# A second layer norm's statistics on ACT, and the softmax denominator's sum and reciprocal on POOL

## The chip, the cores and the metric

The kernel runs on one core of a Trainium2 chip. Its engines are named as the profile names them: PE (TensorE, matmuls and transposes), DVE (VectorE), ACT (ScalarE), POOL (GpSimd) and SP (SyncE, which issues the DMAs). Each works through its own queue in the order written, and waits on semaphores for the others. The metric is the device time of one execution in microseconds (us), the median of three timed runs.

## What is computed

The input is x of 8 x 1024 x 128. Each of the two halves of the block normalises, works, and adds a gated result to x. In the reference, cut to what matters here:

```python
h = _layernorm(x, axis=-1) * (1 + ca) + sa
# for each of 8 heads of 16 columns, over a causal window of 64 positions:
dist = sqrt((diff * diff * m_h).sum(-1) + 1e-08); dist = where(mask, dist, inf)
neg_d, loc = top_k(-dist, 32)
infl = exp(-topd)
infl = infl / (infl.sum(axis=-1, keepdims=True) + 1e-08)        # the softmax denominator
context = einsum('btk,btkd->btd', infl, neighbor_v)
context = context + gate * 0.1 * heb_ctx
out = q_h * context
x = x + ga * (out_sparse @ decoder)
h = _layernorm(x, axis=-1) * (1 + cb) + sb                      # the second layer norm
x = x + gb * _L0_ffn_ref(h, ...)
```

with `_layernorm(x) = (x - mean) / sqrt(var + 1e-5)` over the 128 columns.

## The kernel before, in words

A first part (to about 100 us) normalises x, makes the transposed projections of all 8192 rows and keeps them in SBUF. The main part goes over 64 chunks (`NCH`) of 128 rows each. Each engine has its own `step(i)`, called for i from -3 to 66, in which `k = i + off` names the chunk that an operation works on: several chunks are under way at once. `there(i, off)` says whether that chunk exists, and `s`, `s4` are its buffer of two or of four. The order of the work on each engine is written out by hand by the order of these blocks; nothing reorders it.

One chunk goes this way. SP copies rows into `hst`, `tst`, `sst`. PE multiplies `sqs` and `selm` into norms (L1239, L1241, group `pn`), which ACT copies to `nst` (L752) and `n2` (L758). PE's `distances` (L1149, L1152) fill PSUM; ACT takes two relus of them (L666, L667), DVE joins the third piece into `key` (L998), ACT raises `key` by Ln and Exp (L701, L719). DVE then picks the 32 nearest of each 64 by four rounds of MAX8 (`maxes`, L965) and MATCH_REPLACE8 (`replaces`, L976) for eight heads, into `work`. ACT squares and exponentiates `work` by halves (L628, L635), POOL unfolds it (`big`, L452), PE transposes it (L1168), ACT copies it (L642), PE multiplies it with the values into the contexts (L1182). ACT copies these by two halves of the partitions to `cst` (L713, L714).

In `cst` the last column of each head, `cst[:, s, :, HD]`, is the softmax's sum of weights. DVE adds 1e-8 to it (`den`, L1013) and takes the reciprocal (`rden`, L1026). POOL makes `t1` = context times q (L481), `t2` = the Hebbian part (L483, L485), later `t1` times `rden` (L461) and `osp` = their sum (L465). PE transposes it (L1199) and multiplies with the decoder onto x (L1209, L1210), and ACT copies that sum to `x2` (L706). Then comes the second layer norm: DVE takes BN_STATS (`st_c`, L1007) and BN_AGGR (`mv_c`, L1019), which gives mean and variance of each row; ACT makes `lv_c` = Ln(var + eps), `nm_c` = -mean, `rs_c` = Exp(-lv/2), `nb_c` = nm times rs and `n_c`, the normalised rows (L724, L725, L727, L740, L746). PE transposes them (L1251), ACT scales them to `h2T` (L658), PE multiplies with the chunk's expert matrix (L1190, L1191), ACT copies the result to `yo` (L673) and SP stores it.

On POOL, behind `t1` and `t2`, stand `selm` (L491, an operand of the norms of chunk i + 3), `hsc` (L497), `sst` (L502) and two operations on `n2` (L509, L510).

Of the kernel before, what the change touches and what calls it, by code (L numbers as in the profile page):

```python
# [7 lines left out]
ALU = mybir.AluOpType  # L8
ACT = mybir.ActivationFunctionType
# [4 lines left out]
P = 128  # L14
NB, T, D = 8, 1024, 128
NH, HD = 8, 16
# [13 lines left out]
EPS_LN = 1e-5  # L30
# [47 lines left out]
def adaln_block(nc, x, encq, encv, w1, b1, w2, b2, base, hebu, hebv, dec, wr, amat, bmat, cin, wmod, consts, out):  # L78
    ctx = ExitStack()

    def sb(name, shape, dt=F32):
        return ctx.enter_context(nc.sbuf_tensor(name, shape, dt))

    def sem(name):
        return ctx.enter_context(nc.semaphore(name))

    with ctx:
# [20 lines left out]
        unf = con[:, C_UNF:C_UNF + 2 * WIN].rearrange("p (v j) -> p v j", v=2)  # L108
        ident_bf = sb("ident_bf", [P, P], BF16)
        mask_bf = sb("mask_bf", [P, SW], BF16)  # L110
        bias = sb("bias", [P, 4])

        hT_all = sb("hT_all", [P, NB * TP])
        qT_all = sb("qT_all", [P, NG, NB * TP])
# [48 lines left out]
        den = sb("den", [P, 2, NH])  # L163
# [11 lines left out]
        oT = sb("oT", [P, 2, CH])  # L175
        xs = sb("xs", [P, 4, D])
        x2 = sb("x2", [P, 2, D])
        st_c = sb("st_c", [P, 6])
        mv_c = sb("mv_c", [P, 2, 2])
        lv_c = sb("lv_c", [P, 1])  # L180
        nm_c = sb("nm_c", [P, 1])
        nb_c = sb("nb_c", [P, 1])
# [115 lines left out]
        att_ready = sem("att_ready")  # L298
        xs_in = [sem(f"xs_in{i}") for i in range(4)]
        x2_ready = sem("x2_ready")  # L300
        stc_ready = sem("stc_ready")
        mvc_ready = sem("mvc_ready")
        lnc_done = sem("lnc_done")
        nc_ready = sem("nc_ready")
        pn2_ready = sem("pn2_ready")
# [5 lines left out]
        def need(eng, s, value):  # L311

            if value > 0:
                eng.wait_ge(s, value)
# [12 lines left out]
        def there(i, off):  # L327

            return 0 <= i + off < NCH
# [70 lines left out]
        def _(pool):  # L400
# [5 lines left out]
                ins.then_inc(pool_chain, 1)  # L406
                pool.wait_ge(pool_chain, links[0])

            for col, value in enumerate((EPS_LN, 1e-8, 1.0, 0.0)):
                nc.gpsimd.memset(bias[:, col:col + 1], value).then_inc(bias_set, 1)  # L410
            nc.gpsimd.memset(udiag[:], 0.0).then_inc(ones_set, 1)
            for s in range(4):
# [31 lines left out]
            def step(i):  # L444
                def unfold(w):

                    k, s = i - 1, (i - 1) % 2
                    if there(i, -1):
                        need(pool, wt_ready, 8 * (k - 2) + 4 * w + 4)
                        pool.wait_ge(wsel_ready, 2 * k + 1 + w)  # L450
                        heads = slice(4 * w, 4 * w + 4)
                        nc.gpsimd.tensor_tensor(  # L452
                            wun[:, s, heads].rearrange("p h (v j) -> p h v j", v=2),
                            work[:, s].rearrange("p (h j) -> p h j", h=NH)[:, heads].unsqueeze(2).broadcast_to([P, 4, 2, WIN]),
                            unf.unsqueeze(1).broadcast_to([P, 4, 2, WIN]), ALU.mult).then_inc(w_ready, 1)

                k, s = i - 2, (i - 2) % 2
                if there(i, -2):
                    pool.wait_ge(rden_ready, k + 1)
                    pool.wait_ge(t1_done, k + 1)  # L460
                    nc.gpsimd.tensor_tensor(t1[:].rearrange(h3, h=NH), t1[:].rearrange(h3, h=NH), rden[:, s].unsqueeze(2).broadcast_to([P, NH, HD]), ALU.mult).then_inc(ctx_done, 1)  # L461
                    need(pool, po_ready, k - 1)
                    pool.wait_ge(t2_done, 2 * (k + 1))
                    pool.wait_ge(ctx_done, k + 1)
                    nc.gpsimd.tensor_tensor(osp[:, s], t1[:], t2[:], ALU.add).then_inc(osp_ready, 1)  # L465

                unfold(0)

                unfold(1)

                k, s = i + 3, (i + 3) % 2
                if there(i, 3):
                    win = qT_all[:, :, bass.ds(column(k), 3 * WIN)]
                    need(pool, pn_ready, k - 1)
                    nc.gpsimd.tensor_tensor(sqs[:, s], win, win, ALU.mult).then_inc(opnd_ready, 1)

                k, s, s4 = i - 1, (i - 1) % 2, (i - 1) % 4
                if there(i, -1):
                    q, hb = qh[:, s4, :, 0:HD], qh[:, s4, :, HD:2 * HD]
                    pool.wait_ge(cst_ready, 2 * (k + 1))  # L480
                    nc.gpsimd.tensor_tensor(t1[:].rearrange(h3, h=NH), cst[:, s, :, 0:HD], q, ALU.mult).then_inc(t1_done, 1)  # L481
                    pool.wait_ge(hsc_done, k + 1)
                    nc.gpsimd.tensor_tensor(t2[:].rearrange(h3, h=NH), hb, hsc[:, s].unsqueeze(2).broadcast_to([P, NH, HD]), ALU.mult).then_inc(t2_done, 1)  # L483
                    pool.wait_ge(t2_done, 2 * k + 1)
                    nc.gpsimd.tensor_tensor(t2[:].rearrange(h3, h=NH), t2[:].rearrange(h3, h=NH), q, ALU.mult).then_inc(t2_done, 1)  # L485

                k, s = i + 3, (i + 3) % 2
                if there(i, 3):
                    if i == FIRST:
                        pool.wait_ge(aS_ready, 1)  # L490
                    nc.gpsimd.tensor_tensor(selm[:, s], seln, aS[:, :, bass.ds(k // CPB, 1)].broadcast_to([P, NG, NH]),  # L491
                                            ALU.mult).then_inc(opnd_ready, 1)

                k, s, s4 = i, i % 2, i % 4
                if there(i, 0):
                    pool.wait_ge(rnn_ready, k + 1)
                    nc.gpsimd.tensor_tensor(hsc[:, s], gat[:, s4], rnn[:, s], ALU.mult).then_inc(hsc_done, 1)  # L497

                k, s = i + 3, (i + 3) % 2
                if there(i, 3):  # L500
                    need(pool, dist_ready, k - 1)
                    nc.gpsimd.tensor_tensor(sst[:, s, :, 0:3 * WIN], qT_all[:, :, bass.ds(column(k), 3 * WIN)],  # L502
                                            aS[:, :, bass.ds(k // CPB, 1)].broadcast_to([P, NG, 3 * WIN]), ALU.mult).then_inc(s_ready, 1)

                k, s4 = i + 2, (i + 2) % 4
                if there(i, 2):
                    need(pool, n2_ready, k + 1)
                    need(pool, rnn_ready, k - 3)
                    nc.gpsimd.tensor_scalar(gat[:, s4], n2[:, s4], GATE2, 0.1, ALU.is_gt, ALU.mult).then_inc(n2g_ready, 1)  # L509
                    nc.gpsimd.tensor_scalar(n2g[:, s4], n2[:, s4], 1e-18, None, ALU.max).then_inc(n2g_ready, 1)  # L510
# [15 lines left out]
        def _(act):  # L526
# [1 line left out]
            act.wait_ge(c_in, 32)  # L528

            nc.scalar.activation(ec[:], c_sb[:], ACT.Exp, scale=-1.0).then_inc(ec_ready, 1)  # L530
            act.wait_ge(bias_set, 4)

            def logvar(n, u):
                act.wait_ge(mv_ready, 4 * n + 4)
# [87 lines left out]
            def step(i):  # L622
# [80 lines left out]
                k, s = i - 2, (i - 2) % 2  # L703
                if there(i, -2):
                    act.wait_ge(att_ready, k + 1)
                    nc.scalar.activation(x2[:, s], pAtt, ACT.Copy).then_inc(x2_ready, 1)  # L706

                k, s = i - 1, (i - 1) % 2
                if there(i, -1):
# [3 lines left out]
                    nc.scalar.activation(cst[0:WIN, s], pc[0:WIN, :, 0], ACT.Copy).then_inc(cst_ready, 1)  # L713
                    nc.scalar.activation(cst[WIN:P, s], pc[WIN:P, :, 1], ACT.Copy).then_inc(cst_ready, 1)  # L714

                k, s = i + 1, (i + 1) % 2
                if there(i, 1):
                    act.wait_ge(ln_done, k + 1)
# [1 line left out]

                k, s = i - 2, (i - 2) % 2
                if there(i, -2):
                    act.wait_ge(mvc_ready, k + 1)
                    nc.scalar.activation(lv_c[:], mv_c[:, s, 1:2], ACT.Ln, bias=bias[:, 0:1]).then_inc(lnc_done, 1)  # L724
                    nc.scalar.activation(nm_c[:], mv_c[:, s, 0:1], ACT.Copy, scale=-1.0).then_inc(nm_done, 1)  # L725
                    act.wait_ge(lnc_done, k + 1)
                    nc.scalar.activation(rs_c[:, s:s + 1], lv_c[:], ACT.Exp, scale=-0.5).then_inc(rs_done, 1)  # L727

                k, s4 = i + 2, (i + 2) % 4
                if there(i, 2):  # L730
# [4 lines left out]

                k, s = i - 2, (i - 2) % 2
                if there(i, -2):
                    act.wait_ge(nm_done, k + 1)
                    act.wait_ge(rs_done, k + 1)
                    nc.scalar.activation(nb_c[:], nm_c[:], ACT.Identity, bias=bias[:, 3:4], scale=rs_c[:, s:s + 1]).then_inc(nb_done, 1)  # L740

# [22 lines left out]
        def _(dve):  # L764
# [214 lines left out]
            def step(i):  # L979
# [21 lines left out]
                replaces(i, 2, 0)  # L1001
                replaces(i, 2, 1)

                k, s = i - 2, (i - 2) % 2
                if there(i, -2):
                    dve.wait_ge(x2_ready, k + 1)
                    v.bn_stats(st_c[:], x2[:, s]).then_inc(stc_ready, 1)  # L1007

                k, s = i - 1, (i - 1) % 2
                if there(i, -1):  # L1010
                    dve.wait_ge(cst_ready, 2 * (k + 1))
                    need(dve, rden_ready, k - 1)
                    v.tensor_scalar(den[:, s], cst[:, s, :, HD], 1e-8, None, ALU.add).then_inc(den_done, 1)  # L1013

                k, s = i - 2, (i - 2) % 2
                if there(i, -2):
                    need(dve, stc_ready, k + 1)
                    need(dve, nc_ready, k - 1)
                    v.bn_aggr(mv_c[:, s], st_c[:]).then_inc(mvc_ready, 1)  # L1019

                maxes(i, 3)
                replaces(i, 3, 0)
                k, s = i - 1, (i - 1) % 2
                if there(i, -1):
                    dve.wait_ge(den_done, k + 1)
                    v.reciprocal(rden[:, s], den[:, s]).then_inc(rden_ready, 1)  # L1026

                replaces(i, 3, 1)

            steps(step, routing)  # L1030
# [269 lines left out]
```

## Time and profile before

| | |
|---|---|
| median of 3 timed runs | 841.48 us (840.1 to 842.94) |
| the profiled execution | 845.14 us, of which the span of instructions is 843.4 |
| busy, share of the span | DVE 94%, PE 85%, ACT 73%, PEld 70%, POOL 55% |
| granted TensorE clock, mean | 0.958 |
| main part, from the first `st_c` to the slow tail | 126.0 to about 805 us |
| one repetition (one chunk) there | 11.32 us |

Busy time is the time in which an engine has an instruction of its own under way; PEld is PE's loading of weights, beside its matmuls. A row of a timeline gives the start in us from the start of the span, the time it took, engine, line, operation and operands, and in brackets how long the engine was idle before it and which engine's instruction released it. Instructions on DVE, ACT and POOL overlap a little at their ends, so that two starts can be closer than the first instruction is long. In the last 38 us the granted clock of PE is half, which the page's line on the clock shows.

### The profile page before, as it was taken

What the parts mean: (1) busy time and instruction counts of PE and PEld (TensorE: products, weight loads), DVE (VectorE), ACT (ScalarE), POOL (GpSimd) and SP (SyncE); (2) the same over time, 40 slices, a digit from 0 to 9 for tenths busy, and PEclk for the clock granted to TensorE, in tenths of its full rate; (3) what the DMA queues carried; (4) which work ended last, traced back from release to release, by engine and by line L of the source; (5) the groups of instructions that cost most, each with busy time, mean ns of one, the idle gap of its engine ahead of it and who ended that gap; (6) DMA issues with size and microseconds to landing.
All of it is one profiled execution on the core that took longest, in us unless ns stands there. A gap on an engine that the chain in (4) does not pass through costs nothing.

```text
span 843.4 us, 21229 instructions
## 1 busy us (share of the span) xinstructions
PE 718.6 (85%) x4437; PEld 586.2 (70%) x4437; DVE 788.9 (94%) x6746; ACT 619.5 (73%) x1862; POOL 463.0 (55%) x871
## 2 busy tenths in 40 slices
PE   5997989888888888888888888888888888888845
PEld 3445677777777777777777777777777777777744
DVE  5855999999999999999999999999999999999980
ACT  3981368787777878777777877777878777787853
POOL 2112456666556566655656665565566655656541
PEclk9996989999999999999999999999999999999955
DMA  5310001101111110011110001111100111111000
GB/s 165 102 32 10 24 24 30 30 20 32 31 31 31 29 30 24 27 31 30 32 30 29 26 24 32 31 31 30 30 29 21 31 31 31 31 30 30 18 4 9
DMA packets 49232, 27.24 MB, mean 32 GB/s; under 512 B 5512, under 2 KB 48592, under 8 KB 49104
## 3 DMA queue, kind: packets, MB, share of 16 engines
q1 hardware_dynamic: 49104, 25.90, 10.4%
q8 instruction: 36, 0.59, 0.3%
q14 instruction: 92, 0.75, 0.3%
HBM read 10.28 MB, written 4.19 MB: 17 GB/s over the span
## 4 chain that ended last, share of the span: by engine, by line
DVE 83%; PE 10%; DMA 2%; ACT 2%; issue 2%; POOL 1%; SPq 1%; ACTq 0%; POOLq 0%
DVE work L976 44%; DVE m L965 29%; DVE key L998 4%; DMA big<-in_x 2%; DVE st_c L1007 1%; PE psD L1152 1%; DVE mv_c L1019 1%; PE psC L1182 1%; DVE key L787 1%; PE psD L1057 1%; DVE st_p L778 1%; PE psC L1085 1%; PE psW L1239 1%; DMA wmod_sb<-in_wmod 1%; PE psW L1168 1%
## 5 line engine op out<-in xcount | busy, mean ns | idle before, releaser
L976 DVE MATCH_REPLACE8 work<-m,work 128x64 f32<-128x64 f32 x1536 | 301.8, 208 | 0.0
L1152 PE MATMUL psD<-sst,tst 128*128 128x224 f32 x1024 | 238.9, 356 | 0.0
L965 DVE MAX8 m<-work 128x8 f32<-128x64 f32 x1536 | 209.9, 209 | 0.0
L1152 PEld LDWEIGHTS psD<-sst,tst 128*128 128x128 f32 x1024 | 196.3, 192 | 3.2 <-issue 0.3
L452 POOL TENSOR_TENSOR big<-work,con 128x512 f32<-128x512 f32 x128 | 162.2, 1291 | 13.0 <-ACT work L635 12.9
L481 POOL TENSOR_TENSOR t<-cst,qh 128x128 f32<-128x128 f32 x64 | 27.8, 434 | 232.3 <-ACT cst L714 232.3
L1182 PE MATMUL psC<-vst,big 128*128 128x34 f32 x1024 | 129.0, 272 | 0.0
L1182 PEld LDWEIGHTS psC<-vst,big 128*128 128x128 f32 x1024 | 128.4, 197 | 0.2
L976 DVE MATCH_VALUE_LOAD work<-m,work 128x8 f32 x1536 | 120.0, 78 | 0.0
L976 DVE MATCH_REPLACE8 work<-m,key 128x64 f32<-128x64 f32 x512 | 100.2, 208 | 0.0
L1149 PE MATMUL psD<-mask_bf,ident_bf 128*128 128x448 bf16 x256 | 91.1, 356 | 9.3 <-DMA tst<-nst 1.8
L701 ACT ACTIVATE key<-key,bias 128x512 f32<-128x512 f32 x64 | 46.2, 721 | 69.5 <-DVE key L998 69.5
L1168 PE MATMUL psW<-con,big 128*128 128x128 f32 x512 | 80.0, 280 | 2.9 <-POOL big L452 2.9
L642 ACT ACTIVATE big<-psW 128x512 f32<-128x512 f32 x128 | 76.1, 595 | 3.1 <-PE psW L1168 3.0
L1239 PE MATMUL psW<-sqs,selm 128*8 128x192 f32 x256 | 53.4, 332 | 22.6 <-POOL selm L491 22.6
L965 DVE MAX8 m<-key 128x8 f32<-128x64 f32 x512 | 70.4, 208 | 0.0
L1190 PE MATMUL psX<-x,con 128*128 128x128 f32 x128 | 32.5, 337 | 37.1 <-ACT h2T L658 37.1
L724 ACT ACTIVATE lv_c<-mv_c,bias 128x1 f32<-128x1 f32 x64 | 18.8, 294 | 59.9 <-DVE mv_c L1019 59.9
L1168 PEld LDWEIGHTS psW<-con,big 128*128 128x128 f32 x512 | 58.5, 144 | 4.4 <-POOL big L452 4.1
L1190 PEld LDWEIGHTS psX<-x,con 128*128 128x128 f32 x128 | 19.9, 195 | 59.2 <-ACT h2T L658 59.2
L502 POOL TENSOR_TENSOR sst<-qT_all,aS 128x384 f32<-128x384 f32 x64 | 53.1, 829 | 12.7 <-PE psD L1152 12.7
L635 ACT ACTIVATE work<-work 128x256 f32<-128x256 f32 x128 | 53.3, 417 | 4.1
(199 smaller groups left out, 1474.7 us busy)
## 6 DMA issues: line engine op xcount, KB each, us to landing
hst<-hT_all SPq DMA_DIRECT2D x64, 96.0 KB
tst<-qT_all SPq DMA_DIRECT2D x256, 17.0 KB
big<-in_x SPq DMA_DIRECT2D x16, 256.0 KB, 2.8
tst<-nst SPq DMA_DIRECT2D x256, 1.0 KB
xs<-in_x SPq DMA_DIRECT2D x64, 64.0 KB, 1.9
out<-yo SPq DMA_DIRECT2D x64, 64.0 KB, 1.7
sst<-nst SPq DMA_DIRECT2D x128, 3.0 KB
con<-in_consts SPq DMA_DIRECT2D x1, 549.5 KB, 5.8
```

The source lines that it names most:

```text
L452: nc.gpsimd.tensor_tensor(wun[:, s, heads].rearrange("p h (v j) -> p h v j", v=2), work[:, s].rearrange("p (h j) -> p h j", h=NH)[:, heads ...
L502: nc.gpsimd.tensor_tensor(sst[:, s, :, 0:3 * WIN], qT_all[:, :, bass.ds(column(k), 3 * WIN)], aS[:, :, bass.ds(k // CPB, 1)].broadcast_to( ...
L635: nc.scalar.activation(wk, wk, ACT.Exp, scale=-1.0).then_inc(wsel_ready, 1)
L642: nc.scalar.activation(wts[:, (i - 1) % 2, 4 * w:4 * w + 4].rearrange("p h t -> p (h t)"), psW[:, w], ACT.Copy).then_inc(wts_ready, 1)
L965: last = v.max(m8[:, h], src[:, h * WIN:(h + 1) * WIN])
L976: last = v.match_replace(work[:, s, cols], m8[:, h], src[:, cols], GONE)
L1149: mm(bank_of(r)[:, :, 0:SW], ident_bf[:], mask_bf[:].unsqueeze(1).broadcast_to([P, NG, SW]), start=True, stop=False, skip_group_check=True)
L1152: last = mm(bank_of(r)[:, g, 0:SW], tst[:, s, r, g], sst[:, s, g], start=False, stop=(g == NG - 1), skip_group_check=True)
L1168: nc.tensor.transpose(psW[:, w, (h % 4) * P:(h % 4 + 1) * P], wun[:, s, h], ident).then_inc(wt_ready, 1)
L1182: last = mm(pC[:, h * 2 * VD:(h + 1) * 2 * VD], wts[:, s, h], vst[:, s4, h].rearrange("p v e -> p (v e)"), start=True, stop=True)
L1190: mm(pY, ident, x2[:, s], start=True, stop=False)
L1239: mm(pN, selm[:, s, g], sqs[:, s, g], start=(g == 0), stop=(g == NG - 1))
```

## The change

The second layer norm's statistics are no longer taken on DVE. ACT's copy to `x2` becomes an Identity with `accum_out`, which gives the sum of the row; `nm_c` = -sum/128; a new ACTIVATE `Square` of `x2` with bias `nm_c` and `accum_out` gives the sum of squares about the mean, `ssq_c`, and `lv_c` = Ln(ssq/128 + eps). The pieces `nm_c`, `Square`, `lv_c`, `rs_c` are spread over three places between the copies of `cst` and `n_c`. An ACTIVATE with `accum_out` is followed by a second instruction that reads the accumulator, as the two at L565 in the first part are. The softmax's `den` goes to POOL, ahead of `t1`; its reciprocal becomes a TENSOR_TENSOR with the operation `pow` against a column of -1, on POOL behind `t1`. One more memset makes that column. PE's and SP's code is unchanged.

```diff
@@ pool, step
                     pool.wait_ge(cst_ready, 2 * (k + 1))
+                    need(pool, ctx_done, k - 1)
+                    nc.gpsimd.tensor_scalar(den[:, s], cst[:, s, :, HD], 1e-8, None, ALU.add).then_inc(den_done, 1)
                     nc.gpsimd.tensor_tensor(t1[:].rearrange(h3, h=NH), cst[:, s, :, 0:HD], q, ALU.mult).then_inc(t1_done, 1)
+                    pool.wait_ge(den_done, k + 1)
+                    nc.gpsimd.tensor_tensor(rden[:, s], den[:, s], bias[:, 4:5].broadcast_to([P, NH]), ALU.pow).then_inc(rden_ready, 1)
                     pool.wait_ge(hsc_done, k + 1)
@@ act, step
                     act.wait_ge(att_ready, k + 1)
-                    nc.scalar.activation(x2[:, s], pAtt, ACT.Copy).then_inc(x2_ready, 1)
+                    nc.scalar.activation(x2[:, s], pAtt, ACT.Identity, bias=bias[:, 3:4],
+                                         accum_out=sum_c[:, s:s + 1]).then_inc(x2_ready, 1)
...
+                    act.wait_ge(x2_ready, k + 1)
+                    nc.scalar.activation(nm_c[:], sum_c[:, s:s + 1], ACT.Copy, scale=-1.0 / D).then_inc(nm_done, 1)
...
-                    act.wait_ge(mvc_ready, k + 1)
-                    nc.scalar.activation(lv_c[:], mv_c[:, s, 1:2], ACT.Ln, bias=bias[:, 0:1]).then_inc(lnc_done, 1)
-                    nc.scalar.activation(nm_c[:], mv_c[:, s, 0:1], ACT.Copy, scale=-1.0).then_inc(nm_done, 1)
-                    act.wait_ge(lnc_done, k + 1)
-                    nc.scalar.activation(rs_c[:, s:s + 1], lv_c[:], ACT.Exp, scale=-0.5).then_inc(rs_done, 1)
+                    act.wait_ge(nm_done, k + 1)
+                    nc.scalar.activation(sq_c[:], x2[:, s], ACT.Square, bias=nm_c[:], accum_out=ssq_c[:]).then_inc(ssq_done, 1)
...
-                    act.wait_ge(nm_done, k + 1)
+                    act.wait_ge(ssq_done, k + 1)
+                    nc.scalar.activation(lv_c[:], ssq_c[:], ACT.Ln, bias=bias[:, 0:1], scale=1.0 / D).then_inc(lnc_done, 1)
+                    act.wait_ge(lnc_done, k + 1)
+                    nc.scalar.activation(rs_c[:, s:s + 1], lv_c[:], ACT.Exp, scale=-0.5).then_inc(rs_done, 1)
@@ dve, step
-                    dve.wait_ge(x2_ready, k + 1)
-                    v.bn_stats(st_c[:], x2[:, s]).then_inc(stc_ready, 1)
...
-                    dve.wait_ge(cst_ready, 2 * (k + 1))
-                    need(dve, rden_ready, k - 1)
-                    v.tensor_scalar(den[:, s], cst[:, s, :, HD], 1e-8, None, ALU.add).then_inc(den_done, 1)
...
-                    need(dve, stc_ready, k + 1)
-                    need(dve, nc_ready, k - 1)
-                    v.bn_aggr(mv_c[:, s], st_c[:]).then_inc(mvc_ready, 1)
...
-                    dve.wait_ge(den_done, k + 1)
-                    v.reciprocal(rden[:, s], den[:, s]).then_inc(rden_ready, 1)
```

What stands in a row on POOL in a chunk of the main part, before, from `sqs` to `hsc`:

```order
L475 TENSOR_TENSOR sqs<-qT_all 128x384 [waits pn_ready]
L481 TENSOR_TENSOR t<-cst,qh 128x128 [waits cst_ready]
L483 TENSOR_TENSOR t<-qh,hsc 128x128 [waits hsc_done]
L485 TENSOR_TENSOR t<-t,qh 128x128 [waits t2_done]
L491 TENSOR_TENSOR selm<-con,aS 128x16
L497 TENSOR_TENSOR hsc<-gat,rnn 128x8 [waits rnn_ready]
```

and the same place on POOL now:

```order
L475 TENSOR_TENSOR sqs<-qT_all 128x384 [waits pn_ready]
L482 TENSOR_SCALAR den<-cst 128x8 [waits ctx_done,cst_ready]
L483 TENSOR_TENSOR t<-cst,qh 128x128
L485 TENSOR_TENSOR rden<-den,bias 128x8 [waits den_done]
L487 TENSOR_TENSOR t<-qh,hsc 128x128 [waits hsc_done]
L489 TENSOR_TENSOR t<-t,qh 128x128 [waits t2_done]
L495 TENSOR_TENSOR selm<-con,aS 128x16
L501 TENSOR_TENSOR hsc<-gat,rnn 128x8 [waits rnn_ready]
```

`selm` now has two more instructions between itself and `cst`.

On ACT, before, from the copy to `x2` to the first `Square` of the next chunk's `work`:

```order
L706 ACTIVATE x<-psX 128x128 [waits att_ready]
L713 ACTIVATE cst<-psC 64x136 [waits osp_ready,c_ready]
L714 ACTIVATE cst<-psC 64x136
L719 ACTIVATE key<-key 128x512 [waits ln_done]
L724 ACTIVATE lv_c<-mv_c,bias 128x1 [waits mvc_ready]
L725 ACTIVATE nm_c<-mv_c 128x1
L727 ACTIVATE rs_c<-lv_c 128x1 [waits lnc_done]
L733 ACTIVATE vst<-psW 128x16x16 [waits c_ready,v_ready]
L740 ACTIVATE nb_c<-nm_c,bias,rs_c 128x1 [waits rs_done,nm_done]
L746 ACTIVATE n_c<-x,nb_c,rs_c 128x128 [waits pn2_ready,nb_done]
L752 ACTIVATE nst<-psW 8x192 [waits rows_in1,pn_ready]
```

and the same place on ACT now:

```order
L710 ACTIVATE x,sum_c<-psX,bias 128x128 [waits att_ready]
L718 ACTIVATE cst<-psC 64x136 [waits osp_ready,c_ready]
L719 ACTIVATE cst<-psC 64x136
L724 ACTIVATE nm_c<-sum_c 128x1 [waits x2_ready]
L729 ACTIVATE key<-key 128x512 [waits ln_done]
L734 ACTIVATE sq_c,ssq_c<-x,nm_c 128x128 [waits nm_done]
L740 ACTIVATE vst<-psW 128x16x16 [waits c_ready,v_ready]
L746 ACTIVATE lv_c<-ssq_c,bias 128x1 [waits ssq_done]
L748 ACTIVATE rs_c<-lv_c 128x1 [waits lnc_done]
L750 ACTIVATE nb_c<-nm_c,bias,rs_c 128x1 [waits rs_done]
L756 ACTIVATE n_c<-x,nb_c,rs_c 128x128 [waits pn2_ready,nb_done]
L762 ACTIVATE nst<-psW 8x192 [waits rows_in0,pn_ready]
```

`Square` has come in, `lv_c` and `rs_c` stand behind `vst`, and the wait for `mvc_ready` is gone.

## Rows read from the trace of the kernel before

**Rows 1.** Windows: one repetition; PE, PEld, DVE, ACT, POOL busy; clock; DMA share; GB/s.

```profile
408.91:420.23 11.32, 9.94 (x67) 8.41 (x66) 11.32 (x103) 8.90 (x27) 7.00 (x14) 1.00 0.10 30
```

**Rows 2.** The page's chain that ended last, by engine.

```profile
DVE 83%; PE 10%; DMA 2%; ACT 2%; issue 2%; POOL 1%; SPq 1%; ACTq 0%; POOLq 0%
```

**Rows 3.** That chain in order of time: start, time in the chain, engine, line.

```profile
408.91 0.20 DVE st_c L1007
409.11 0.07 DVE den L1013
409.18 0.15 DVE mv_c L1019
...
411.10 0.06 DVE rden L1026
...
420.23 0.20 DVE st_c L1007
```

**Rows 4.** Timeline of ACT over one repetition.

```profile
399.95 0.40 ACT L628 ACTIVATE work<-work 128x256 f32<-128x256 f32 x1
...
405.17 0.21 ACT L696 ACTIVATE rnn<-lnn 128x8 f32<-128x8 f32 x1
406.38 0.72 ACT L701 ACTIVATE key<-key,bias 128x512 f32<-128x512 f32 x1 [1.00 <-DVE key L998]
407.01 0.26 ACT L706 ACTIVATE x<-psX 128x128 f32<-128x128 f32 x1
407.17 0.26 ACT L713 ACTIVATE cst<-psC 64x136 f32<-64x136 f32 x1
407.46 0.28 ACT L714 ACTIVATE cst<-psC 64x136 f32<-64x136 f32 x1
...
409.36 0.29 ACT L724 ACTIVATE lv_c<-mv_c,bias 128x1 f32<-128x1 f32 x1 [0.98 <-DVE mv_c L1019]
...
411.01 0.30 ACT L752 ACTIVATE nst<-psW 8x192 f32<-8x192 f32 x1
...
411.27 0.40 ACT L628 ACTIVATE work<-work 128x256 f32<-128x256 f32 x1
```

**Rows 5.** Timeline of POOL and PE in the same repetition.

```profile
405.53 0.98 PE L1182 MATMUL psC<-vst,big 128*128 128x34 f32 x8
...
407.81 0.44 POOL L481 TENSOR_TENSOR t<-cst,qh 128x128 f32<-128x128 f32 x1 [3.55 <-ACT cst L714]
...
409.10 0.21 POOL L491 TENSOR_TENSOR selm<-con,aS 128x16 f32<-128x16 f32 x1
...
409.37 0.82 PE L1239 MATMUL psW<-sqs,selm 128*8 128x192 f32 x4 [0.37 <-POOL selm L491]
...
410.11 0.61 PE L1241 MATMUL psW<-con,sqs 128*128 128x8 f32 x4
```

**Rows 6.** All `st_c` (first and last start), and one `den` in the slow tail.

```profile
L1007 DVE BATCH_NORM_STATS2 st_c<-x x64: 273/284/298, 126.0 to 836.6; 128x6 f32<-128x128 f32 x64
...
817.33 0.17 DVE L1013 TENSOR_SCALAR den<-cst 128x8 f32<-128x8 f32 x1 [1.50 <-ACT cst L714]
```

**Rows 7.** Groups of instructions: count | busy us, mean ns of one | idle before.

```profile
L658 ACT ACTIVATE h2T<-psX,modT 128x128 f32<-128x128 f32 x64 | 28.2, 441 | 1.2 <-PE psX L1251 1.1
L565 ACT ACTIVATION_READ_ACCUMULATOR qT_all<-psD,con 128x1 f32 x32 | 7.0, 220 | 0.0
L497 POOL TENSOR_TENSOR hsc<-gat,rnn 128x8 f32<-128x8 f32 x64 | 13.0, 204 | 0.0
L509 POOL TENSOR_SCALAR gat<-n 128x8 f32<-128x8 f32 x64 | 16.2, 253 | 5.7 <-ACT n L758 0.4
L452 POOL TENSOR_TENSOR big<-work,con 128x512 f32<-128x512 f32 x128 | 162.2, 1291 | 13.0 <-ACT work L635 12.9
L965 DVE MAX8 m<-work 128x8 f32<-128x64 f32 x1536 | 209.9, 209 | 0.0
L965 DVE MAX8 m<-key 128x8 f32<-128x64 f32 x512 | 70.4, 208 | 0.0
```

More of the change, by code:

```diff
@@ L110, in adaln_block @@
         mask_bf = sb("mask_bf", [P, SW], BF16)
-        bias = sb("bias", [P, 4])
+        bias = sb("bias", [P, 5])
         hT_all = sb("hT_all", [P, NB * TP])
@@ L177, in adaln_block @@
         x2 = sb("x2", [P, 2, D])
-        st_c = sb("st_c", [P, 6])
-        mv_c = sb("mv_c", [P, 2, 2])
+        sum_c = sb("sum_c", [P, 2])
+        ssq_c = sb("ssq_c", [P, 1])
+        sq_c = sb("sq_c", [P, D])
         lv_c = sb("lv_c", [P, 1])
@@ L300, in adaln_block @@
         x2_ready = sem("x2_ready")
-        stc_ready = sem("stc_ready")
-        mvc_ready = sem("mvc_ready")
+        ssq_done = sem("ssq_done")
         lnc_done = sem("lnc_done")
@@ L407, in link @@
                 pool.wait_ge(pool_chain, links[0])
-            for col, value in enumerate((EPS_LN, 1e-8, 1.0, 0.0)):
+            for col, value in enumerate((EPS_LN, 1e-8, 1.0, 0.0, -1.0)):
                 nc.gpsimd.memset(bias[:, col:col + 1], value).then_inc(bias_set, 1)
@@ L530, in _ @@
             nc.scalar.activation(ec[:], c_sb[:], ACT.Exp, scale=-1.0).then_inc(ec_ready, 1)
-            act.wait_ge(bias_set, 4)
+            act.wait_ge(bias_set, 5)
             def logvar(n, u):
@@ L714, in step @@
                     nc.scalar.activation(cst[WIN:P, s], pc[WIN:P, :, 1], ACT.Copy).then_inc(cst_ready, 1)
+                k, s = i - 2, (i - 2) % 2
+                if there(i, -2):
+                    act.wait_ge(x2_ready, k + 1)
+                    nc.scalar.activation(nm_c[:], sum_c[:, s:s + 1], ACT.Copy, scale=-1.0 / D).then_inc(nm_done, 1)
                 k, s = i + 1, (i + 1) % 2
@@ L1002, in step @@
                 replaces(i, 2, 1)
-                k, s = i - 2, (i - 2) % 2
-                if there(i, -2):
-                    dve.wait_ge(x2_ready, k + 1)
-                    v.bn_stats(st_c[:], x2[:, s]).then_inc(stc_ready, 1)
-                k, s = i - 1, (i - 1) % 2
-                if there(i, -1):
-                    dve.wait_ge(cst_ready, 2 * (k + 1))
-                    need(dve, rden_ready, k - 1)
-                    v.tensor_scalar(den[:, s], cst[:, s, :, HD], 1e-8, None, ALU.add).then_inc(den_done, 1)
-                k, s = i - 2, (i - 2) % 2
-                if there(i, -2):
-                    need(dve, stc_ready, k + 1)
-                    need(dve, nc_ready, k - 1)
-                    v.bn_aggr(mv_c[:, s], st_c[:]).then_inc(mvc_ready, 1)
                 maxes(i, 3)
                 replaces(i, 3, 0)
-                k, s = i - 1, (i - 1) % 2
-                if there(i, -1):
-                    dve.wait_ge(den_done, k + 1)
-                    v.reciprocal(rden[:, s], den[:, s]).then_inc(rden_ready, 1)
                 replaces(i, 3, 1)
```

## Prediction

> **What bounds the kernel now.** I read four views, in this order. First the busy time of the engines over one repetition in the middle of the run. DVE is busy 11.32 of 11.32 us there, PE 9.94, ACT 8.90, POOL 7.00 [rows 1]. One repetition is the distance from one `st_c` to the next, 420.23 - 408.91 = 11.32 us [rows 3]. Second the chain that ended last by engine: 83% DVE [rows 2]. Third that chain in order of time: through the repetition it never leaves DVE, and the four instructions that the change takes away stand in it with 0.20 (`st_c`), 0.07 (`den`), 0.15 (`mv_c`) and 0.06 us (`rden`) [rows 3]. These are shares by which they hold up the next one, smaller than the instructions' own times because DVE starts the next before the last has ended. Fourth the timelines of ACT, POOL and PE, for how near the other engines are to a bound of their own [rows 4, 5]. So anything that shortens DVE pays at once, until the next loop through the other engines is as long.
>
> **What DVE gives up.** 0.20 + 0.07 + 0.15 + 0.06 = 0.48 us in each repetition. Nothing waits in their place: MAX and MATCH_REPLACE follow each other as they do in the other rounds. DVE alone could run at 11.32 - 0.48 = 10.84 us. The first `st_c` is at 126.0 [rows 6]; from there to 805, where the slow tail begins, are 60 repetitions of 11.32. The bound of the gain is 60 x 0.48 = 28.8 us.
>
> **What ACT takes.** ACT sits idle 1.00 us for `key` from DVE and 0.98 us for `mv_c` from DVE in each repetition [rows 4]. The second wait goes, for `nm_c` now comes from ACT's own sum. Added: the `x2` copy becomes an Identity with a bias column and a sum. An ACTIVATE with two columns is 0.44 long (`h2T`), the copy of the same size 0.26; with one column I take the middle, +0.1, and the read of the accumulator is 0.22 [rows 4, 7]. `Square` is a new 128x128 ACTIVATE of at most 0.44 with another 0.22. Together 0.1 + 0.22 + 0.44 + 0.22 = 1.0 us, and 8.90 + 1.0 = 9.9 is under 10.84. The four small ones (`nm_c`, `lv_c`, `rs_c`, `nb_c`) stay, and only move. What hides this work is the idle time that ACT has; were that gone, the 1.0 us would all show. On the order within ACT: `x2` stands ahead of the two `cst` copies and now delays them by about 0.3 - 0.1 = 0.2 us. In the repetition shown, the first `cst` starts at 407.17, while the products that it reads end at 405.53 + 0.98 = 406.51 [rows 4, 5], so it is ACT, not PE, that sets `cst` now.
>
> **What POOL takes, and the loop on which it lies.** POOL waits for the second `cst` until 407.81, and has its own idle time ahead of that (3.55 us) [rows 5]; by its busy share two small instructions are free. By its place they are not. Behind the new `den` and power stand `t1`, `t2` and `selm`; PE waits for `selm` (0.37 idle) before the norms' matmuls, ACT's `nst` copy waits for those, and on ACT the whole next repetition, `Square` of `work` first, queues behind `nst`. That closes a loop: work (ACT) - yo (ACT) - transposes and contexts (PE) - cst (ACT) - POOL - pn (PE) - nst - work. Its length with no wait for DVE in it, from the rows:
> from `work` at 399.95 to the end of the second half of the contexts at 406.51, 6.56 [rows 4, 5] (this stretch is dense: from ACT's `yo` on PE has no pause, and ACT's own way, 5.43 to the end of `rnn`, then 0.63 for `key`, 0.16 + 0.23 for `x2`, is 6.45 and hidden behind it); 0.05 to `cst`, 0.29 + 0.28 for the two copies: 7.18; 0.07 to POOL, then 409.10 + 0.21 - 407.81 = 1.50 to the end of `selm`: 8.75; 0.06 to PE, 410.11 + 0.61 - 409.37 = 1.35 for the norms: 10.16; 0.03 to `nst` and 411.27 - 411.01 = 0.26 to `work`: 10.45 us [rows 4, 5]. Before, this is 0.87 us under DVE's 11.32 and costs nothing. Now `den` adds the 0.25 of a TENSOR_SCALAR 128x8, less the 0.04 by which POOL's instructions overlap, 0.21; and the power adds p - 0.04, where p is its duration [rows 5, 7]. The loop becomes **10.62 + p**, against 10.84 for DVE.
>
> **The price of the power.** No power on any engine is in the trace. From below: the same shape with a multiply takes 0.20 us (`hsc`), p = 0.20 [rows 7]. From above, 16 times as many multiplies take 0.44 us (`t1`), 64 times as many 1.29 us (`unfold`) [rows 5, 7]. Less than 0.20 I exclude, since that is what POOL takes for the lightest operation of this shape. A power is many operations on each element; I take the row of 16 multiplies as nearest, p = 0.43, and keep 0.20 and 1.29 as ends. Then the loop is 11.05 us, longer than DVE's 10.84, and it sets the pace: 60 x (11.32 - 11.05) = 16.2 us gained.
>
> **The tail.** Behind 805 us the statistics chain of the last chunks lies bare, as DVE's wait of 1.50 us for `cst` shows [rows 6]. There about 0.35 us on DVE per chunk give way to the sum's read, `Square` and its read, 0.22 + 0.44 + 0.22, so some 0.5 us more, three times: +1.5 us. In the head nothing is removed from the chain that I can see. The sum for the profiled execution: span 843.4 - 16.2 + 1.5 = 828.7. It took 845.1 us, and the median of the three timed runs is 841.5; on that I put the difference of -14.7: **826.8 us**.
>
> **A rule that speaks against it.** MAX8 takes 209 ns when it reads `work` and 208 when it reads `key`, in rounds beside which POOL works and in rounds beside which it idles [rows 7], so POOL and DVE do not slow each other in the rows that count. The Trainium skill, page "Perfetto Trace Analysis", section "Optimizing Scalar/DVE Operations", warns that GpSimd and DVE share an SBUF read port, so that moving work between these two might not help. If it acted here the two tiny operations would lose part of DVE's gain; that is the contention rival below.
>
> **Rivals.** (1) DVE stays the bound. The power costs no more than 0.22 us: 10.84 us, 28.8 - 1.5 = 27.3 gained, 814.2 us. For it: 8 elements a partition, and the row of the multiply. Against: only if a power is as cheap as a multiply. Chance 0.22. (2) The power is dear, on the other side: one mechanism, POOL's `den` and power ahead of `selm`, from p = 0.68 on no gain is left (10.62 + 0.68 = 11.30, and the tail). At p = 1.29 the repetition is 11.91: 60 x 0.59 + 1.5 = +36.9, 878 us; at p = 1.0 it is 11.62, +19.5, 861 us. For it: POOL's order, and the 0.37 that PE already waits for `selm`. Against: POOL's fixed share dominates at 8 elements. Chance 0.27. (3) Between them, p from 0.63 to 0.72: within 2.5 us of 841.5; chance 0.08. (4) ACT or a port in the way: ACT's reads of the accumulator cost double, or DVE loses 0.1 to 0.2 us beside POOL. ACT has 10.84 - 9.9 = 0.9 us to spare, so it would have to be 1.9 us and not 1.0; for contention nothing in the rows speaks. It would come out at about 845; chance 0.05. My forecast, p from 0.22 to 0.63, has 0.38.
>
> **How the numbers follow.** A measurement of this kernel tells 0.3%, 2.5 us, from no change. Faster: 0.38 + 0.22 = 0.60. Same: 0.08. Slower: 0.27 + 0.05 = 0.32. The range goes from the DVE bound with 2 us to spare, 812, up to the power at 1.0 us, 860; beyond that I leave about 0.15.
>
> **What would show it.** Right: the repetition is 11.05 us, the distance between two `key` of DVE; DVE has a new wait of some 0.2 us a repetition, on ACT's `qh` or on `key`; ACT's wait for `mv_c` is gone, its wait for `key` nearly so, and there is a new one for `nst` from PE's norms; PE's wait for `selm` grows; the power's row reads about 0.43. Wrong in the first step: DVE is still without a pause, at 10.84. Wrong in the price: the power's row reads other than 0.43, and the repetition is off 10.62 + p. Wrong in the loop: the power's row is near 0.43 and the repetition is not near 11.05; then some stretch that I took as dense had slack in it, or ACT's added work is not hidden.

## The result and the profile after

The changed kernel takes 957.4 us, the median of four runs (955.4 to 959.0), against 842.2 us of the kernel before in runs beside it. The ratio is 1.137, 95% interval 1.133 to 1.141. It is 115.2 us slower; the forecast was 14.7 us faster, with 860 us as the upper end. Both the sign and the range were wrong.

The page of the kernel after: the span, the busy time, two of the lines in 40 slices, and the chain that ended last by engine ("issue" is time in which the engine waited for nothing that the profile shows).

```profile
span 957.0 us, 21168 instructions
...
PE 765.3 (80%) x4437; PEld 634.6 (66%) x4437; DVE 765.0 (80%) x6490; ACT 674.7 (71%) x2054; POOL 583.9 (61%) x1000
...
DVE  5957988888788888788888788787788888878880
...
PEclk9977899988899988899988899889888999988955
...
PE 47%; POOL 23%; ACT 15%; issue 9%; DVE 3%; DMA 2%; SPq 0%; POOLq 0%; ACTq 0%
```

DVE did become lighter, 765.0 us busy instead of 788.9, but it now idles and has 3% of the chain where it had 83% [rows 2]. Two things stand out. POOL is in the chain with 23%. And the granted clock of PE, which before stayed at full from 126 us to the tail, now reads 8 or 9 in the tenths of the page through the main part, 0.92 in the mean from 126 to 900 us.

The costliest groups and the waits of the kernel after (busy us, mean ns of one | idle before, releaser):

```profile
L485 POOL TENSOR_TENSOR rden<-den,bias 128x8 f32<-128x8 f32 x64 | 106.7, 1667 | 0.0
L1228 PE MATMUL psW<-sqs,selm 128*8 128x192 f32 x256 | 53.1, 330 | 105.9 <-POOL selm L495 105.9
L762 ACT ACTIVATE nst<-psW 8x192 f32<-8x192 f32 x64 | 20.5, 320 | 133.3 <-PE psW L1230 133.3
L1008 DVE SCALAR_TENSOR_TENSOR key<-psD,key 128x512 f32<-128x512 f32 x64 | 44.2, 691 | 133.7 <-ACT qh L690 133.6
```

The power takes 1667 ns. The three waits are the loop of the prediction, link by link: PE waits for `selm` from POOL, ACT waits with `nst` for PE, DVE waits with `key` for ACT's `qh`. Here is an undisturbed repetition, one in which PE's granted clock stays at full, on the timelines of POOL, PE, ACT and DVE:

```profile
404.06 0.25 POOL L482 TENSOR_SCALAR den<-cst 128x8 f32<-128x8 f32 x1 [4.10 <-ACT cst L719]
404.27 0.43 POOL L483 TENSOR_TENSOR t<-cst,qh 128x128 f32<-128x128 f32 x1
404.67 1.66 POOL L485 TENSOR_TENSOR rden<-den,bias 128x8 f32<-128x8 f32 x1
406.30 0.40 POOL L487 TENSOR_TENSOR t<-qh,hsc 128x128 f32<-128x128 f32 x1
...
407.19 0.22 POOL L495 TENSOR_TENSOR selm<-con,aS 128x16 f32<-128x16 f32 x1
...
407.46 0.82 PE L1228 MATMUL psW<-sqs,selm 128*8 128x192 f32 x4 [1.77 <-POOL selm L495]
...
408.86 0.32 ACT L762 ACTIVATE nst<-psW 8x192 f32<-8x192 f32 x1 [1.98 <-PE psW L1230]
...
413.56 0.69 DVE L1008 SCALAR_TENSOR_TENSOR key<-psD,key 128x512 f32<-128x512 f32 x1 [1.25 <-ACT qh L690]
...
425.75 0.69 DVE L1008 SCALAR_TENSOR_TENSOR key<-psD,key 128x512 f32<-128x512 f32 x1 [1.25 <-ACT qh L690]
```

From one `key` to the next are 12.19 us where a repetition took 11.32 [rows 3]. Sixty times 0.87 is 52 us, less than half of what was lost. The other part shows when a repetition with full clock is put beside one without (windows; the columns are as in [rows 1]):

```profile
387.62:401.37 13.75, 11.16 (x68) 9.70 (x67) 10.95 (x98) 9.85 (x31) 8.88 (x15) 0.88 0.08 23
401.37:413.56 12.19, 9.77 (x68) 8.32 (x67) 10.95 (x98) 9.63 (x31) 8.90 (x15) 1.00 0.06 18
...
392.00:393.00 1.00, 0.00 (x0) 0.00 (x0) 1.00 (x12) 0.93 (x3) 0.95 (x2) 1.00 0.02 7
393.00:394.00 1.00, 0.28 (x2) 0.19 (x3) 1.00 (x11) 0.12 (x1) 0.97 (x4) 1.00 0.00 0
394.00:395.00 1.00, 1.00 (x8) 0.63 (x6) 1.00 (x11) 0.00 (x0) 0.87 (x2) 0.82 0.00 0
395.00:396.00 1.00, 1.00 (x5) 0.93 (x6) 1.00 (x12) 0.62 (x3) 0.72 (x3) 0.50 0.00 0
```

PE lies still while it waits for `selm` (busy 0.00 in the slice from 392 and 0.28 in the next), and within the slice from 394 its granted clock falls from 2.4 to 1.2 GHz, for about 3.4 us. Such a repetition takes 13.75 us, 1.56 more than the one beside it. Of the 60 repetitions of the main part 38 are of this kind (13.47 to 13.92 us); what they have over 12.19 adds up to 58.6 us. The wait alone doesn't decide it: in the repetition at full clock PE waits for `selm` just as long (the 1.77 us before 407.46), and its clock holds. What decides between the two no run here shows. The matmuls that run at half speed are on the loop, those between `selm` and `nst` and the two groups of distances behind them:

```profile
395.20 0.53 PE L1138 MATMUL psD<-mask_bf,ident_bf 128*128 128x448 bf16 x1
395.53 1.70 PE L1141 MATMUL psD<-sst,tst 128*128 128x224 f32 x4
...
397.61 1.15 PE L1141 MATMUL psD<-sst,tst 128*128 128x224 f32 x4
...
398.79 0.59 ACT L670 ACTIVATE key<-psD 64x512 f32<-64x512 f32 x1 [0.86 <-PE psD L1141]
```

The first group takes 1.70 us and the second, at half clock in part, 1.15 us, where each takes 0.92 at full clock. ACT's `key` starts at 398.79, 0.03 us after the second ends. From `nst` to this `key` are 3.41 us, in the repetition at full clock 2.13 (408.86 to 410.99): 1.28 of the 1.56 us.

### The profile page after: what moved, and what is told of

The parts are those of the page before. It is cut to its first block, busy times and chain, and to the rows that moved or that the text cites. A ratio compares the mean times of both kernels' runs of the same rounds, so it can differ in the third digit from the quotient of the medians.

```text
span 957.0 us, 21168 instructions
## 1 busy us (share of the span) xinstructions
PE 765.3 (80%) x4437; PEld 634.6 (66%) x4437; DVE 765.0 (80%) x6490; ACT 674.7 (71%) x2054; POOL 583.9 (61%) x1000
## 4 chain that ended last, share of the span: by engine, by line
PE 47%; POOL 23%; ACT 15%; issue 9%; DVE 3%; DMA 2%; SPq 0%; POOLq 0%; ACTq 0%
PE psD L1141 12%; PE psC L1171 11%; POOL rden L485 10%; PE psW L1228 4%; PE psW L1157 3%; PE psD L1138 3%; ACT key L671 3%; PE psW L1230 3%; POOL t L483 3%; POOL t L487 2%; PE psX L1198 2%; PE psX L1188 2%; ACT cst L719 2%; ACT yo L677 2%; ACT cst L718 2%
## 5 line engine op out<-in xcount | busy, mean ns | idle before, releaser
L1141 PE MATMUL psD<-sst,tst 128*128 128x224 f32 x1024 | 286.1, 410 | 0.0
L1141 PEld LDWEIGHTS psD<-sst,tst 128*128 128x128 f32 x1024 | 232.6, 228 | 12.0 <-issue 0.3
L482 POOL TENSOR_SCALAR den<-cst 128x8 f32<-128x8 f32 x64 | 16.1, 251 | 245.4 <-ACT cst L719 245.4
L1008 DVE SCALAR_TENSOR_TENSOR key<-psD,key 128x512 f32<-128x512 f32 x64 | 44.2, 691 | 133.7 <-ACT qh L690 133.6
L1228 PE MATMUL psW<-sqs,selm 128*8 128x192 f32 x256 | 53.1, 330 | 105.9 <-POOL selm L495 105.9
L762 ACT ACTIVATE nst<-psW 8x192 f32<-8x192 f32 x64 | 20.5, 320 | 133.3 <-PE psW L1230 133.3
L1228 PEld LDWEIGHTS psW<-sqs,selm 128*8 128x8 f32 x256 | 17.9, 89 | 138.2 <-POOL selm L495 125.7
L485 POOL TENSOR_TENSOR rden<-den,bias 128x8 f32<-128x8 f32 x64 | 106.7, 1667 | 0.0
L1138 PE MATMUL psD<-mask_bf,ident_bf 128*128 128x448 bf16 x256 | 104.1, 406 | 1.8 <-DMA tst<-nst 1.8
L670 ACT ACTIVATE key<-psD 64x512 f32<-64x512 f32 x64 | 37.6, 587 | 46.5 <-PE psD L1141 46.4
```

The lines of the kernel that those rows point to most:

```text
L485: nc.gpsimd.tensor_tensor(rden[:, s], den[:, s], bias[:, 4:5].broadcast_to([P, NH]), ALU.pow).then_inc(rden_ready, 1)
L1008: v.scalar_tensor_tensor(out=e, in0=pH[:, :, WIN:2 * WIN], scalar=0.0, in1=e, op0=ALU.max, op1=ALU.min).then_inc(d2_ready, 1)
L1138: mm(bank_of(r)[:, :, 0:SW], ident_bf[:], mask_bf[:].unsqueeze(1).broadcast_to([P, NG, SW]), start=True, stop=False, skip_group_check=True)
L1141: last = mm(bank_of(r)[:, g, 0:SW], tst[:, s, r, g], sst[:, s, g], start=False, stop=(g == NG - 1), skip_group_check=True)
L1228: mm(pN, selm[:, s, g], sqs[:, s, g], start=(g == 0), stop=(g == NG - 1))
```

## The experiments

All are compared with the kernel before on the same chip. The theory: the whole loss hangs on the power on POOL, by two ways, its duration in the loop, and PE's clock, which falls because PE now waits. The rivals: ACT's sums and `Square` have a share; `den` and the place on POOL cost by themselves; the half clock lies where nothing waits for it.

**One part alone: the layer norm.** The changed kernel with `den` and the reciprocal back on DVE.

```diff
@@ pool, step
-                    nc.gpsimd.tensor_scalar(den[:, s], cst[:, s, :, HD], 1e-8, None, ALU.add).then_inc(den_done, 1)
...
-                    nc.gpsimd.tensor_tensor(rden[:, s], den[:, s], bias[:, 4:5].broadcast_to([P, NH]), ALU.pow).then_inc(rden_ready, 1)
@@ dve, step
+                    v.tensor_scalar(den[:, s], cst[:, s, :, HD], 1e-8, None, ALU.add).then_inc(den_done, 1)
...
+                    v.reciprocal(rden[:, s], den[:, s]).then_inc(rden_ready, 1)
```

> Only the layer norm's statistics go to ACT; den and the reciprocal stay on DVE. Theory (the loss is POOL's power in front of selm): ACT's added work is hidden, DVE gives up 0.35 us a repetition, 11.32 - 0.35 = 10.97 us, clock 1.0 through the main part, 842.2 - 21 + 1.5 = 823 us. Rival (a good part of the loss is ACT's two sums and the Square): slower than 842 us.

Measured: 823.9 us, ratio 0.978 (0.975 to 0.980); 823 was expected. One repetition (windows, as above):

```profile
406.68:417.67 10.99, 9.79 (x68) 8.33 (x67) 10.99 (x100) 9.62 (x30) 7.03 (x13) 1.00 0.12 36
```

DVE is busy for all of the 10.99 us, and ACT for 9.62. The layer norm's half of the change is by itself a gain of 18.6 us, and the work that it adds to ACT is hidden, as reckoned; that rival falls.

**The other part alone: the denominator.** The kernel before with `den` and the power on POOL, in the places of the change (the column of -1 is made as there).

```diff
@@ pool, step
+                    nc.gpsimd.tensor_scalar(den[:, s], cst[:, s, :, HD], 1e-8, None, ALU.add).then_inc(den_done, 1)
...
+                    nc.gpsimd.tensor_tensor(rden[:, s], den[:, s], bias[:, 4:5].broadcast_to([P, NH]), ALU.pow).then_inc(rden_ready, 1)
@@ dve, step
-                    v.tensor_scalar(den[:, s], cst[:, s, :, HD], 1e-8, None, ALU.add).then_inc(den_done, 1)
...
-                    v.reciprocal(rden[:, s], den[:, s]).then_inc(rden_ready, 1)
```

> Only den and the power go to POOL; the layer norm's statistics stay on DVE. Theory: the whole loss is here: an undisturbed repetition of 12.2 us, the same short stretches of half clock on PE, about 955 us. Rival (the two parts share the loss): about 900 us.

Measured: 952.1 us, ratio 1.130 (1.127 to 1.133). The page's line of the clock looks as that of the changed kernel, and a disturbed repetition is as long (windows; 37 of 60 are of this kind):

```profile
PEclk9977899888999988889999888999988989999865
...
398.76:412.54 13.78, 11.20 (x69) 9.70 (x67) 11.31 (x100) 9.25 (x28) 8.88 (x15) 0.88 0.08 24
```

The whole loss is here. Once POOL sets the pace, DVE's relief by the layer norm is worth nothing: the ratio is 1.130 without it and 1.137 with it.

**The power's duration taken away, all else kept.** The changed kernel with a multiply in the power's place.

```diff
-                    nc.gpsimd.tensor_tensor(rden[:, s], den[:, s], bias[:, 4:5].broadcast_to([P, NH]), ALU.pow).then_inc(rden_ready, 1)
+                    nc.gpsimd.tensor_tensor(rden[:, s], den[:, s], bias[:, 4:5].broadcast_to([P, NH]), ALU.mult).then_inc(rden_ready, 1)
```

> The changed kernel with a multiply in place of the power, so that the denominator's division is left out of the result; all instructions, places and waits stay. Theory (loop of 10.62 us + the duration of that one instruction, DVE at 10.84): the instruction takes 0.20 us, the repetition is 10.84 us, no stretch of half clock, 842.2 - 28.8 + 1.5 = 815 us. Rival (the place on POOL, or ACT's work, costs by itself): 842 us or more.

Measured: 814.1 us, ratio 0.966 (0.961 to 0.971). The row of the instruction, and two `key` of DVE, now without a wait:

```profile
L485 POOL TENSOR_TENSOR rden<-den,bias 128x8 f32<-128x8 f32 x64 | 13.0, 204 | 0.0
...
402.95 0.67 DVE L1008 SCALAR_TENSOR_TENSOR key<-psD,key 128x512 f32<-128x512 f32 x1
413.81 0.67 DVE L1008 SCALAR_TENSOR_TENSOR key<-psD,key 128x512 f32<-128x512 f32 x1
```

204 ns and 10.86 us a repetition: the bound of DVE that the prediction put at 10.84 is there. Neither the place on POOL nor `den` costs anything by itself. 143 us lie between this kernel and the changed one, and the only difference is the operation of one instruction on 128x8 elements. (This kernel leaves the denominator's division out of its result.)

**PE kept busy while it waits.** The changed kernel with six more matmuls ahead of the wait for `selm`.

```diff
+                    if there(i, -1):
+                        for _ in range(6):
+                            mm(psD[:, 2, 0:P], ident, ident, start=True, stop=True)
                     pe.wait_ge(opnd_ready, 2 * (k + 1))
```

> The changed kernel with six more 128x128 matmuls per repetition (about 1.6 us) on PE in its wait for selm, into a PSUM bank that is overwritten right after. Theory (of the 115 us lost, some 52 are 60 repetitions of 12.19 instead of 11.32 us and the other 60 are PE at half clock): with PE busy the clock stays at 1.0, every repetition is 12.2 to 12.3 us, about 896 to 902 us, faster than the changed kernel although it does more. Rival (the half clock lies where PE waits anyway and costs nothing; or PE's clock falls all the same): 957 us or more.

Measured: 899.0 us, ratio 1.067 (1.064 to 1.069). It does more work and is 58.4 us faster than the changed kernel. The clock on its page, a repetition in windows, and the added work in PE's timeline:

```profile
PEclk9996999999999999999999999999999999999965
...
402.51:414.77 12.26, 11.19 (x81) 9.89 (x80) 10.95 (x97) 9.71 (x31) 8.89 (x15) 1.00 0.09 27
...
406.75 1.50 PE L1226 MATMUL psD<-con 128*128 128x128 f32 x12
408.68 0.82 PE L1231 MATMUL psW<-sqs,selm 128*8 128x192 f32 x4 [0.43 <-POOL selm L495]
```

The repetitions keep the 12.2 us of the power's loop: from 135 us on none is longer than 12.34. So of the 115 us some 57 are the loop and 58 the half clock, as much as the 38 long repetitions of the changed kernel had over 12.19. PE's wait for `selm` is down from 1.77 to 0.43 us here, and with PE at work in its place the clock holds.

**Half of the power.** The changed kernel with the power on four heads instead of eight.

```diff
+            link(nc.gpsimd.memset(rden[:], 1.0))
...
-                    nc.gpsimd.tensor_tensor(rden[:, s], den[:, s], bias[:, 4:5].broadcast_to([P, NH]), ALU.pow).then_inc(rden_ready, 1)
+                    nc.gpsimd.tensor_tensor(rden[:, s, 0:4], den[:, s, 0:4], bias[:, 4:5].broadcast_to([P, 4]), ALU.pow).then_inc(rden_ready, 1)
```

> The changed kernel with the power on four of the eight heads; the other four keep a divisor of one, which leaves their division out of the result. Theory (the power's time goes by its elements, 1.67 us = 0.20 and some 0.18 for each of eight): 0.93 us for four, a repetition of 10.52 + 0.93 = 11.45 us, 842.4 + 60 x 0.13 + 1.5 = 852 us where the clock holds, up to 15 us more where it falls now and then. Rival (the power has a large fixed cost): about 1.6 us still, and 950 us.

Measured: 856.3 us, ratio 1.016 (1.013 to 1.019). The row of the power, the one with PE's wait for `selm`, and a repetition:

```profile
L486 POOL TENSOR_TENSOR rden<-den,bias 128x4 f32<-128x4 f32 x64 | 66.4, 1038 | 0.0
...
L1229 PE MATMUL psW<-sqs,selm 128*8 128x192 f32 x256 | 53.4, 332 | 69.0 <-POOL selm L496 69.0
...
363.41:374.97 11.56, 9.77 (x68) 8.32 (x67) 10.95 (x97) 9.62 (x31) 8.26 (x15) 1.00 0.10 29
```

1038 ns for four and 1667 for eight elements a partition: by a line through these two, 157 ns for each, and some 0.41 us beside. My split (0.20 fixed, 0.18 each) gave 0.93 us and was a tenth low; the rival of a constant 1.6 us falls. 11.56 - 1.04 = 10.52 and 12.19 - 1.67 = 10.52: the loop without the power is 10.52 us, twice the same. The clock stays at full here, though PE waits for `selm` in this kernel too, 69.0 us over 60 repetitions or 1.15 us in each, where the changed kernel has 105.9 us or 1.77. A new wait of PE can thus cost its length alone.

**The power behind `selm`.** The changed kernel with the power moved to another place on POOL.

```diff
-                    pool.wait_ge(den_done, k + 1)
-                    nc.gpsimd.tensor_tensor(rden[:, s], den[:, s], bias[:, 4:5].broadcast_to([P, NH]), ALU.pow).then_inc(rden_ready, 1)
...
                     nc.gpsimd.tensor_tensor(selm[:, s], seln, aS[:, :, bass.ds(k // CPB, 1)].broadcast_to([P, NG, NH]),
                                             ALU.mult).then_inc(opnd_ready, 1)
+                    pool.wait_ge(den_done, k + 1)
+                    nc.gpsimd.tensor_tensor(rden[:, s], den[:, s], bias[:, 4:5].broadcast_to([P, NH]), ALU.pow).then_inc(rden_ready, 1)
```

> The changed kernel with the power behind selm on POOL instead of ahead of t2. Theory: the loop through selm is relieved, but hsc, sst, the two on n2, t1 times rden, osp and the unfolding stand behind the power, and the unfolding closes the next loop: with 1.63 us in it, it starts some 13.3 us after the first Square, so the repetition is still about 12.1 us, and PE still waits; 930 to 955 us. Rival (only the place ahead of selm was bad): the repetition falls to 10.84 us, about 815 us.

Measured: 979.9 us, ratio 1.164 (1.159 to 1.169), 25 us above my upper end. The clock, the new wait of PE, and a repetition of the disturbed kind:

```profile
PEclk9978989889777788888777778888777778888755
...
PE psW L1160 <- POOL big L452: 57.2, 69, 1.3
...
410.48:425.98 15.50, 14.86 (x73) 12.74 (x71) 11.04 (x97) 9.86 (x31) 9.09 (x16) 0.69 0.07 20
```

PE waits for the unfolded weights (`big`) instead of `selm`, as the theory has it. From 246 us on the repetitions alternate between 11.8 and 15.5 us. The undisturbed one is shorter than the changed kernel's, by 0.4 us, and the kernel slower, since the clock is half for a longer part: in the repetition shown it reads 0.50 from 410 to 420 us, without a break. It falls there behind two waits for `big`, of 1.20 and 0.48 us, and PE is busy through all of these 10 us. What the 28 long repetitions have over 11.81 adds up to 98.6 us. The place ahead of `selm` was not the fault: with 1.67 us in it, POOL's row closes a loop in this place too. What the clock makes of it, I did not foresee in size.

**Both parts off DVE, without the power.** The changed kernel with `den` and the power taken off POOL, and the denominator as Exp(-Ln(sum + 1e-8)) on ACT.

```diff
@@ act, step, behind the Square
+                    act.wait_ge(cst_ready, 2 * (k + 1))
+                    nc.scalar.activation(den[:, s], cst[:, s, :, HD], ACT.Ln, bias=bias[:, 1:2]).then_inc(den_done, 1)
@@ act, step, behind vst
+                    act.wait_ge(den_done, k + 1)
+                    need(act, ctx_done, k - 1)
+                    nc.scalar.activation(rden[:, s], den[:, s], ACT.Exp, scale=-1.0).then_inc(rden_ready, 1)
```

> Both halves off DVE and none on POOL: the layer norm's statistics on ACT as changed, the denominator as Exp(-Ln(sum + 1e-8)), two ACTIVATEs of 128x8 on ACT behind the Square and behind vst. Theory: ACT has the room, its way from cst to nst grows by 0.4 us and its loop is 10.81 us, just under DVE's 10.84: 815 us, faster than e1_ln_only by 8. Rival (ACT becomes the bound): 0.2 to 0.4 us a repetition more, 825 to 840 us.

Measured: 819.3 us, ratio 0.970 (0.966 to 0.974). Two `key` of DVE, and ACT's two waits that it had in [rows 4], of which one is left:

```profile
406.27 0.68 DVE L1015 SCALAR_TENSOR_TENSOR key<-psD,key 128x512 f32<-128x512 f32 x1
417.12 0.68 DVE L1015 SCALAR_TENSOR_TENSOR key<-psD,key 128x512 f32<-128x512 f32 x1
...
406.98 0.72 ACT L701 ACTIVATE key<-key,bias 128x512 f32<-128x512 f32 x1 [0.59 <-DVE key L1015]
```

10.85 us a repetition: DVE is the bound again, and ACT still has 0.59 us to wait for it. This version is the fastest of those that compute everything, 4.6 us under the layer norm alone (the intervals of the two ratios do not touch) and 23 us under the kernel before. The remaining 4 us over my 815 lie ahead of the repetitions, for the most part: the first `key` is at 86.47 us here and at 83.15 with the multiply, the last at 775.29 and 772.00. The change doesn't touch that first part, and two of the six runs of this kernel took 812 us, the other four 819 to 820. Where this comes from stays open.

## Why the prediction was wrong, point by point

- **What bounds the kernel, and what DVE gives up**: right. DVE without the four instructions repeats every 10.85 us where 10.84 was said, and with only the statistics gone 10.99 (10.97 by the same rows).
- **What ACT takes**: right in kind and size. The copy with a sum grew from 258 to 349 ns, the reads of the accumulator are 190 and 187, `Square` 387 ns: 0.85 us in place of 1.0, of which ACT's busy time in a repetition shows 0.73 (9.63 against 8.90), and hidden.
- **The loop through `selm`**: right. It was put at 10.62 us + p and is 10.52 us + p, for two values of p.
- **The price of the power: the step that failed.** I took p = 0.43 us and kept 1.29 as the upper end; it is 1.67. The bound from above was none: I counted a power as up to 64 multiplies of the same instruction, but the rows of a multiply say nothing of how many steps a power takes. Measured, one element a partition costs 157 ns, where the multiply goes from 204 ns for 8 to 434 for 128 elements, 1.9 ns each: by these numbers a power is worth some 80 multiplies, and has 0.2 us more beside. With p = 1.67 the formula gives 12.29 us and 60 x 0.97 + 1.5 = +60 us, about 902, which is what the kernel with PE kept busy takes (899).
- **A term that was put at nothing without a reason: PE's clock.** Forecast and rivals let PE wait longer and never asked what its clock does then. In the kernel before PE is busy 9.94 of 11.32 us and the clock holds; in the changed kernel it lies still for 1.8 us behind POOL in each repetition and runs at 1.2 GHz for 3.4 us in 38 of 60, in the loop that is already too long. That is the other 58 us. The trace of before had a sign of it: the tail runs at half clock, and so does PE in the head from 60 to 80 us, where it is busy 15.78 of 20 us and its granted clock reads 0.50.
- **The rival on the other side** had the first half of the mechanism, the place and the point of decision, with a chance of 0.27. Its dearest case, 878 us, was still 79 us short, since it had neither the price nor the clock. With the price bounded from one side only, it deserved more, and the range should have been open upward.
- **The contention rival**: nothing came of it. The prediction quotes for it the Trainium skill, page "Perfetto Trace Analysis", section "Optimizing Scalar/DVE Operations", that moving work between GpSimd and DVE might not help because they share a read port. No slowing of this kind shows here: DVE's MATCH_REPLACE stays at 208 ns in the changed kernel, and with the multiply in place of the power DVE runs at its bound.
- **The signs to look for**: the wait for `nst` behind PE's norms, DVE's for `qh` and PE's longer one for `selm` all came; the sign "the power's row reads other than 0.43 and the repetition is off 10.62 + p" is the case for the first half only, since the repetition at full clock follows p.

## What to carry to other kernels

An operation that the trace has never shown has no upper bound from other operations of its shape: before it goes into a loop that had 0.87 us to spare (10.45 against 11.32), run it once by itself. Where a move relieves the bound engine, price the place on the engine that takes it, not its idle share: POOL was 38% idle and the two instructions still set the pace, because PE and ACT stand behind them. And a new wait on PE is to be priced twice, once by its length alone, as it came out with half of the power, and once with the matmuls behind it at half clock, here 1.56 us more in 38 of 60 repetitions.

## What the runs showed of the hardware that I had not expected

- A power of 128x8 on POOL takes 1667 ns, of 128x4 1038 ns, a multiply of 128x8 204 ns.
- PE's granted clock fell from 2.4 to 1.2 GHz for about 3.4 us in 38 of 60 repetitions of a loop in which PE was busy 9.77 of 12.19 us at full clock and waited 1.77 us at a stretch; in repetitions of 11.56 us (PE busy 9.77, waiting 1.15 us for `selm`) it held. With the power behind `selm` it stayed at 1.2 GHz for 10 us on end, though PE was busy through all of them.
- Six useless matmuls a repetition, in the place of a wait, made a kernel 58 us faster; its clock held in every repetition of the main part.
